# First attention layer of a two-layer cross-attention kernel: the weighted sum moved to directly behind the scores, all three probability groups turned and split in their own slot

## What is computed

```python
a = _layer_norm(audio_kv, ln_gamma, ln_beta)
Q = (hidden_states @ Wq.T).reshape(B, Tt, HEADS, HEAD_DIM).transpose(0, 2, 1, 3)
K = (a @ Wk.T).reshape(B, Ta, HEADS, HEAD_DIM).transpose(0, 2, 1, 3)
V = (a @ Wv.T).reshape(B, Ta, HEADS, HEAD_DIM).transpose(0, 2, 1, 3)
scores = jnp.einsum('bhtd,bhsd->bhts', Q, K) * scale
scores = jnp.where(mask, scores, jnp.float32(-jnp.inf))
attn = jax.nn.softmax(scores, axis=-1)
out = jnp.einsum('bhts,bhsd->bhtd', attn, V)
return hidden_states + jnp.tanh(gate) * (out.reshape(B, Tt, D) @ Wo.T)
```

## Time and profile before

| | us |
|---|---|
| median of three runs | 1791.48 (1789.04 to 1791.99) |
| the profiled execution | 1799.13 |
| its span | 1797.3 |
| TensorE busy in the span | 1672.9 (93%) |
| VectorE busy | 1203.6 (67%) |
| ScalarE busy | 1041.9 (58%) |
| GpSimd busy | 902.7 (50%) |
| DMA queue of SP, share of 16 engines | 28.4% |

### The profile page before, as it was taken

How to read it: one execution, slowest core, us unless ns; L and a number is a source line. 1 busy time by engine, 2 the same in 40 slices (tenths; PEclk the granted TensorE clock), 3 DMA queues, 4 the chain that set the end, 5 groups by cost and what they waited for, 6 DMA issues and landing times.

```text
span 1797.3 us, 36860 instructions
## 1 busy us (share of the span) xinstructions
PE 1672.9 (93%) x12520; PEld 1576.3 (88%) x12520; DVE 1203.6 (67%) x2340; ACT 1041.9 (58%) x2023; POOL 902.7 (50%) x655
## 2 busy tenths in 40 slices
PE   4788988997899999999999999999999999999997
PEld 3677877786789999999999987889999999999986
DVE  5577777777356766766766766466676677677673
ACT  2467766676264655656656555545665656556563
POOL 4456665542144545536535547453653554455483
PEclk8899999999699999999999999899999999999998
DMA  7967666746221111111211114221121121120031
GB/s 211 234 161 183 180 173 177 179 115 167 73 81 62 54 50 37 64 41 36 70 35 36 70 32 131 62 85 37 36 70 36 35 70 36 36 70 1 2 91 40
DMA packets 109995, 150.81 MB, mean 84 GB/s; under 512 B 25540, under 2 KB 95684, under 8 KB 109828
## 3 DMA queue, kind: packets, MB, share of 16 engines
q1 hardware_dynamic: 108484, 142.45, 28.4%
q10 hardware_dynamic: 1344, 6.19, 1.0%
HBM read 108.32 MB, written 3.42 MB: 62 GB/s over the span
## 4 chain that ended last, share of the span: by engine, by line
PE 67%; DVE 10%; ACT 3%; issue 2%; SPq 1%; POOL 1%; DMA 1%; ACTq 0%; DVEq 0%; POOLq 0%
PE ps L770 12%; PE ps L772 11%; PE ps L771 11%; PE ps L1025 7%; PE ps L1029 7%; PE ps L1027 7%; PE ps L960 2%; DVE ar L1866 2%; PE ps L1005 2%; PE ps L992 1%; DVE neg L1742 1%; PE ps L853 1%; PE ps L870 1%; DVE ar L1911 1%; ACT prob L1299 1%
## 5 line engine op out<-in xcount | busy, mean ns | idle before, releaser
L722 POOL TENSOR_TENSOR rr<-ar,rr 125x512 fp32r<-125x512 f32 x336 | 455.3, 1387 | 406.6 <-ACT rr L1483 398.7
L1025 PE MATMUL ps<-cx,rr 125*128 125x258 f32 x1344 | 396.6, 295 | 0.0
L1029 PE MATMUL ps<-cx,rr 125*128 125x258 f32 x1344 | 379.6, 282 | 0.0
L1027 PE MATMUL ps<-cx,rr 125*128 125x256 f32 x1344 | 379.3, 282 | 0.0
L770 PE MATMUL ps<-rr,ct 128*125 128x256 f32 x1152 | 329.6, 286 | 4.5 <-DVE ar L1911 2.7
L772 PE MATMUL ps<-rr,ct 128*125 128x256 f32 x1152 | 324.7, 282 | 0.0
L771 PE MATMUL ps<-rr,ct 128*125 128x256 f32 x1152 | 324.7, 282 | 0.0
L1470 ACT ACTIVATE ar<-ar 125x512 f32<-125x512 f32 x336 | 208.5, 626 | 84.5 <-DVE ar L1911 59.4
L1027 PEld LDWEIGHTS ps<-cx,rr 125*128 125x128 f32 x1344 | 254.9, 190 | 0.0
L1029 PEld LDWEIGHTS ps<-cx,rr 125*128 125x128 f32 x1344 | 254.8, 190 | 0.0
L1025 PEld LDWEIGHTS ps<-cx,rr 125*128 125x128 f32 x1344 | 253.6, 189 | 0.1
(11 more groups left out here) (210 smaller groups left out, 3778.6 us busy)
## 6 DMA issues: line engine op xcount, KB each, us to landing
raw_t<-in_ctx_t SPq DMA_DIRECT2D x24, 1500.0 KB, 6.7
k<-khl SPq DMA_DIRECT2D x192, 187.5 KB
raw<-in_ctx SPq DMA_DIRECT2D x16, 1500.0 KB
raw<-in_ctx SPq DMA_DIRECT2D x8, 1408.0 KB
raw<-stat_scratch ACTq DMA_DIRECT2D x7, 750.0 KB, 3.9
w_raw<-in_wq SPq DMA_DIRECT2D x32, 128.0 KB, 2.3
w_raw<-in_wk SPq DMA_DIRECT2D x32, 128.0 KB, 2.2
qo<-in_wqt SPq DMA_DIRECT2D x32, 128.0 KB, 3.2
```

Of the source, the lines that this page charges most:

```text
L722: pool.tensor_tensor(group(p[:, 1, :, :], u, k), x, f(group(p[:, 0, :, :], u, k)), ALU.subtract)\
L1025: pe.matmul(ps[:, bank, 0:D + 2], hi, cx[0:KC, c, 0:D + 2], start=c == 0, stop=False, skip_group_check=True)
L1027: pe.matmul(ps[:, bank, 0:D], hi, cx[0:KC, c, D + 2:CW], start=False, stop=False, skip_group_check=True)
L1029: mm = pe.matmul(ps[:, bank, 0:D + 2], lo, cx[0:KC, c, 0:D + 2], start=False, stop=c == CH - 1, skip_group_check=True)
```

## The change

In each slot, TensorE does the weighted sum of g-1 directly behind the scores of g+1, then turns 0 and 1 of g, then the key block, then the third turn of g itself, then the value block. ScalarE: value copy, output of g-1, high parts 0 and 1 of g, softmax of g+1, third high part of g, key copy. VectorE: maximum, low values, collapse, low parts 0 and 1, statistics (now at the end of slots 0, 1 and 2), third low part of g. GpSimd scales the second half of batch b+2 in slot 5 ahead of key block 5 instead of behind it. The statistics' turn in slot 3 goes back to bank 7 and waits for the collapse; in slot 4 the wait for its copy stands ahead of the weighted sum. Ahead of the slots, the statistics of batch 1 come behind the split of the first context, its turn behind key block 3 instead of 1, its spreading behind the last key copy instead of the fourth, and SP's load of raw for batch 1 behind all constants. Behind the slots, one third turn and one third high and low part go away, since they are done in their own slot.

```diff
@@ SP @@
                     n_const += 1
-                    if n_const == 10:
-
-                        sp.wait_ge(s["bn_done"], 3)
-                        load_raw(0, 1)
...
             constants()
+            sp.wait_ge(s["bn_done"], 3)
+            load_raw(0, 1)
@@ GpSimd @@
             def slot(b, t, n, kind):
                 if kind == "full" and t == 2:
                     variance(b + 2)
+                if kind == "full" and t == 5:
+                    scale(b + 2, 1)
...
-                    if t in (4, 5):
-                        scale(b + 2, t - 4)
+                    if t == 4:
+                        scale(b + 2, 0)
@@ TensorE @@
                 if t or later:
-                    transposes(g - 1, (t - 1) % SLOTS, 2)
+                    if t == 4 and kind == "full":
+                        pe.wait_ge(s["stat_row"], b + 3)
+                    weighted(b if t else b - 1, (t - 1) % SLOTS, g - 1, n if t else 1 - n)
+                transposes(g, t, 0)
+                transposes(g, t, 1)
                 if t in K_AT and kind != "plain":
                     u = K_N[t]
                     pe.wait_ge(s["zks"], 6 * (b + 1) + u)
-                    if t == 4 and kind == "full":
-                        pe.wait_ge(s["stat_row"], b + 3)
                     keys(b + 1, u, *K_AT[t], 5)
-                if t or later:
-                    weighted(b if t else b - 1, (t - 1) % SLOTS, g - 1, n if t else 1 - n)
-                transposes(g, t, 0)
-                transposes(g, t, 1)
+                transposes(g, t, 2)
                 if t == 3 and kind == "full":
-
-                    pe.wait_ge(s["zks"], 6 * (b + 1) + 4)
-                    turn_stats(b + 2, 5)
+                    pe.wait_ge(s["zoc"], g)
+                    turn_stats(b + 2)
...
                 keys(0, n, *K_FIRST[n], (5, 3)[n % 2])
-                if n == 1:
+                if n == 3:
                     pe.wait_ge(s["stat_row"], 1)
                     turn_stats(1)
...
             whole_batches(pe, slot, "full", "keys", "plain")
-            transposes(GT0 - 1, SLOTS - 1, 2)
             weighted(B - 1, SLOTS - 1, GT0 - 1, 1)
@@ ScalarE @@
-                if t or later:
-                    high_probs(g - 1, 2)
                 if u_last is not None and (t or later) and not (kind == "plain" and t):
...
-                if t in K_AT and kind != "plain":
-                    u = K_N[t]
-                    act.wait_ge(s["zkl"], 6 * (b + 1) + u - 4)
-                    keys(b + 1, u, 5)
+                if t or later:
+                    output(g - 1)
+                high_probs(g, 0)
+                high_probs(g, 1)
                 if kind == "full" and t == 4:
                     spread_stats(b + 2)
...
                     softmax(n if t < SLOTS - 1 else 1 - n, (t + 1) % SLOTS, g + 1)
-                if t or later:
-                    output(g - 1)
-                high_probs(g, 0)
-                high_probs(g, 1)
+                high_probs(g, 2)
+                if kind == "full" and t == 3:
+                    turn_stats(b + 2)
+                if t in K_AT and kind != "plain":
+                    u = K_N[t]
+                    act.wait_ge(s["zkl"], 6 * (b + 1) + u - 4)
+                    keys(b + 1, u, 5)
...
                 keys(0, n, (5, 3)[n % 2])
-                if n == 1:
+                if n == 3:
                     turn_stats(1)
-                if n == 3:
-                    spread_stats(1)
+            spread_stats(1)
@@ VectorE @@
-            for k in range(3):
-                load_stats(1, k)
             for jc in range(DH):
...
                 low(ct[:, 1, :, v], raw_t[:, :, v], ct[:, 0, :, v]).then_inc(s["zcv"], 1)
+            for k in range(3):
+                load_stats(1, k)
...
-                if t or later:
-                    low_probs(g - 1, 2)
                 if u_last is not None and (t or later) and not (kind == "plain" and t):
                     values(b + 1 if t else b, u_last, 1 - n if t else n, 6)
-                if t == 0 and later:
-                    reciprocals(b - 1, 1 - n)
-                if kind == "full" and t in (1, 2):
-                    load_stats(b + 2, t)
-                if kind == "plain" and t == SLOTS - 1:
-                    reciprocals(b, n)
                 if t or later:
                     collapse(b if t else b - 1, (t - 1) % SLOTS, g - 1)
                 low_probs(g, 0)
                 low_probs(g, 1)
-                if kind == "full" and t == 0:
-                    load_stats(b + 2, 0)
+                if t == 0 and later:
+                    reciprocals(b - 1, 1 - n)
+                if kind == "full" and t < 3:
+                    load_stats(b + 2, t)
+                if kind == "plain" and t == SLOTS - 1:
+                    reciprocals(b, n)
+                low_probs(g, 2)
```

More of the change, by code:

```diff
@@ L776, in _, with turn_stats @@
             drain(pe, 1)
-            def turn_stats(b, bank=7):
+            def turn_stats(b):
                 pe.wait_ge(s["std_ready"], 2 * b + 2)
-                pe.transpose(ps[0:CH, bank, 256:256 + P], mv[:, 1, :], ident[:, :]).then_inc(s["stat_t"], 1)
+                pe.transpose(ps[0:CH, 7, 256:256 + P], mv[:, 1, :], ident[:, :]).then_inc(s["stat_t"], 1)
             pe.wait_ge(s["w0_lo"], 1)
@@ L1252, in _, with turn_stats @@
             high(xs[:, 0, :, :], xt[:, :, :]).then_inc(s["x_hi"], 1)
-            def turn_stats(b, bank=7):
+            def turn_stats(b):
                 act.wait_ge(s["stat_t"], b + 1)
-                act.activation(mv_row[:, :], ps[0:CH, bank, 256:256 + P], ACT.Copy).then_inc(s["stat_row"], 1)
+                act.activation(mv_row[:, :], ps[0:CH, 7, 256:256 + P], ACT.Copy).then_inc(s["stat_row"], 1)
                 wait_apart(act, s["stat_row"], b + 1)
@@ L1354, in slot @@
                     softmax(n if t < SLOTS - 1 else 1 - n, (t + 1) % SLOTS, g + 1)
-                if t or later:
-                    output(g - 1)
-                high_probs(g, 0)
-                high_probs(g, 1)
+                high_probs(g, 2)
[5 more added lines that the diff above has]
+                    keys(b + 1, u, 5)
                 if kind == "full":
-                    if t == 3:
-                        turn_stats(b + 2, 5)
                     if t == 6:
@@ L1403, in _ @@
             whole_batches(act, slot, "full", "keys", "plain")
-            high_probs(GT0 - 1, 2)
             output(GT0 - 1)
@@ L1798, in _ @@
             whole_batches(dve, slot, "full", "keys", "plain")
-            low_probs(GT0 - 1, 2)
             collapse(B - 1, SLOTS - 1, GT0 - 1)
```

## The result

The changed kernel takes 1800.89 us, the median of 20 runs (1791.79 to 1809.42); the kernel before 1791.03 (20 runs, 1788.19 to 1798.48). The ratio is 1.0045, with an interval of 1.0028 to 1.0062: slower by 8 us by the ratio and by 9.9 us by the medians, where 1784.6 was forecast and the range ended at 1797. A second measurement further down gives 1.0056 [1.0035, 1.0078].

The account below looks back on a forecast made before the run. TensorE plus 28.8 us of idle time was taken to bound the slots, then a loop outside them. Start +2.5, loop -7.5, batch 6 +1.2 and batch 7 -3.1 gave -6.9: 1784.6 from 1791.48, range 1777 to 1797.

Parts of the forecast that it names:

- I leave them as they are in the sum: Last two windows, batches 6 and 7: TensorE's missing clock shares, 1.7 and 3.6 us, were kept unchanged.
- Start, "I take +2.5": Ahead of the slots: later statistics of batch 1 delay the start by 2.5 us, bounds 0 and 5.5.
- Key blocks 2 to 5 wait: Ahead of the slots: GpSimd's third context split moves from 36.13 to 41.7, and these blocks wait for it.
- Loop, -7.5: Batch 0's slot 3 to batch 6's slot 1: 275.1 us instead of 282.56.
- T: Time from SP's load of raw to GpSimd's key block 1, read as 25.1 to 28.1 us and taken as unchanged.
- 21.5 + T: Length per batch of the loop outside the slots: 16.8 from statistics' turn to load, 4.7 for block and variance, plus T.
- The paragraph on the rule against it: TensorE's clock: an array that idled runs at half clock until busy again; missing shares are 1.7 and 3.6 us.
- the clock falls where TensorE waits most: Last two windows: the trace's clocks of 0.96 and 0.92 were read as agreeing with the half-clock rule.
- rival (d): TensorE's clock: added idle time drops it, and the missing 5.3 us double, giving 1790; chance 8%.
- rival (b): Loop through raw and k3 gets longer, up to 3.3 us a batch in T, giving 1801; chance 24%.
- Batch 6, +1.2: Batch 6: 43.6 us instead of 42.41, with a 3 us stall for k3 before batch 7's scores.
- Batch 7, -3.1: Batch 7 and the tail: 42.4 us instead of 45.49, with slots of 5.18.

Follow-up runs that it names:

- cut3: Changed kernel with the old order ahead of the slots, GpSimd's variance ahead of key block 1, and the last batch's stacks 0 to 3 released by key block 4: 1783.08, ratio 0.9945.
- cut3b: The same kernel as cut3, measured once more: 1781.85 us, ratio 0.9951 to the kernel before.
- cut2late: Changed kernel with batch 1's variance behind GpSimd's first key block, the slots' variance ahead of key block 1, and earlier last stacks: 1781.61 us, ratio 0.9946.
- oldstart: Changed kernel with the order ahead of the slots of the kernel before: 1795.4 us, ratio 1.0023 to the kernel before.
- newstart: Kernel before with only the changed order ahead of the slots: 1798.55 us, ratio 1.0036 to the kernel before.
- latevar1: Changed kernel with GpSimd's variance of batch 1 moved from ahead of its third context split to behind its first key block: 1791.79 us, ratio 1.0011.
- earlyvar: Changed kernel with GpSimd's variance in the slots queued ahead of key block 1 instead of behind it: 1791.65 us, ratio 1.0005 to the kernel before.
- busyplain: cut3 with eight needless identity turns on TensorE in each of batch 7's slots 0 to 6: 1779.17 us, ratio 0.9922 to the kernel before.
- startvar: Changed kernel with the old order ahead of the slots and GpSimd's variance ahead of key block 1, without earlier last stacks: 1786.29 us, ratio 0.996.
- the second group: Runs of cut3, startvar, newstart and one further kernel beside the kernel before on one chip; ratios 0.9945, 0.996, 1.0036 and 1.0098.

## Why the prediction was wrong

**The step that failed.** The forecast put new waits of TensorE into its sum and left the clock out of it: "I leave them as they are in the sum". Of the 13.3 us between the forecast's -6.9 and the marks' +6.4, the lower clock behind waits, counted by the slots, is 2.35 us in the loop and 4.6 in batch 7 (three slots of 6.7 instead of 5.2), together about half. The rest is waiting itself: the loop's long laps (2.2 us, and 1.1 that the formula misses), a start mis-sized by 1.2, and small differences in batches 6 and 7. How far the losses can be undone is shown by runs (cut3, cut3b, cut2late); the clock's share is read from one profile and only argued.

**The order itself was read right.** The weighted sum's waits are gone, plain slots are 5.18, slot 4 5.42 (5.24 forecast), slots with keys and values 6.1 to 6.3 (6.15), batch 6 41.0 without its stall (40.7). With three edits beside it the order is worth 0.5% (0.9945, 0.9951, 0.9946). What was forecast is thus there, but the change doesn't reach it: three waits, each for something on GpSimd's or SP's list, together took 1% back (the two on GpSimd's list are measured singly, the one for k3 isn't told apart from nothing).

**Start, "I take +2.5": mis-sized, the place named.** VectorE's and GpSimd's scalings of the first context now begin together and take 4.41 and 3.31 us where VectorE's took 2.30 before; the statistics so ended at 40.8 and not 39.0, the third split came at 43.98 and not 41.7. "Key blocks 2 to 5 wait" stood there with no price: 6.87 us of idle TensorE, with the next key matmuls at the lower clock. The marks say +3.7, the runs 0.22% (oldstart), 0.36% (newstart) and 0.34% (latevar1), 4 to 6 us.

**Loop, -7.5: the formula held nearly, its price for a wait did not.** With the T of the changed kernel's own trace, 21.5 + T gives 50.1, 49.7 and 48.0 for batches 2, 3 and 5, and the slots give 47.45 for the other two (46.95 forecast): 242.7 for five, where 240.5 was forecast and 246.1 measured. Of the 3.4 left, 2.35 is the clock: slot 4 at 6.68 and 6.53. The paragraph on the rule against it asked whether the clock falls more in batches 6 and 7, where it already did; it fell in the loop too, at 1.00 before, where the forecast itself put new waits. Its reading that "the clock falls where TensorE waits most" was wrong as well: in the earlier trace rows TensorE is idle for 10% of the first window, at 1.00, and for 7% of the second, at 0.96. What came is rival (d), its 5.3 us against about 7, partly in a place it did not name, beside what rival (b) calls "the loop is longer", but not because T grows (26.7 in the mean, where it decides from 27.9); a single T of 28 costs 2 to 3 us and a T of 25 gives nothing back, since the slots then bind. A mean T in a sum hides this.

**Batch 6, +1.2: about right** (1.7), in part by luck. The stall for k3 was 1.9, not 3, and slot 7 behind it took 7.07 us and not the 6.2 of earlyvar, at the lower clock, which the sum didn't have. From SP's first stack (405.40) to these scores (410.33) it is 4.9 us, where issue and landing had been taken as 5.8.

**Batch 7, -3.1: wrong sign, +2.8.** The count of slots was right: 31.0 us for slots 0 to 5 in cut3b and busyplain, 31.25 before. In the changed kernel it was 35.6 and 36.9, by three and four slots at the lower clock. In the 18 profiles this stretch takes 30.5 to 31.3 in the three that keep the old order throughout, and 31.0 to 37.1 in the thirteen with the new one in batch 7 too. The stall for k3 ahead of it neither suffices nor is needed: the eight of the thirteen that have it took 31.1 to 36.9 (startvar, with a stall of 1.9, ran at full clock), the five without it 31.0 to 37.1 (cut2late). What sets the lower clock off there is open; busyplain speaks, weakly, for the idle time in its own slots.

**The clock in the timed runs.** Over the change's 20 runs, the mean clock is 0.968 to 0.977 with a mean of 0.973; over the 20 runs of the kernel before in the second group it is 0.974 to 0.980, mean 0.977. Over all timed runs, within one kernel, a mean clock lower by 0.001 goes with 1.35 us more. By that the missing 0.004 is some 5 of the 8 to 10 us. It is a correlation, since idle time and lower clock come together, and it isn't the whole price: earlyvar is 7 us faster than the changed kernel with a mean clock of 0.9735, higher by 0.0006 only. The Trainium skill (TensorE: Matmul & The Clock Gate, HAM oscillation — how this bites in real kernels) says that a wait which recurs in a loop, when it is long enough, throttles the array each time anew. The traces agree only in part: the clock fell behind the statistics' turn in four waits (1.81 to 2.83 us) and not in three others (1.57, 2.10 and 2.21).

## What to carry to other kernels

When an order is tightened until a loop outside it binds, price each new wait of TensorE with the work that may run at half clock behind it: here 1.2 us behind a wait of 2.4, where the clock fell. Take the slack per batch and not in the mean, since a short lap of the loop gives nothing back. And look down each in-order queue for one cheap instruction that waits ahead of something urgent: a single variance in GpSimd's list cost 0.34% ahead of the slots, and another 0.40% inside them. Moving it pays only in the order that needs it: in the kernel before, the second move cost 0.32%.

## What was not expected of the hardware

The length of a wait alone doesn't say whether the clock falls behind it: 1.81 us did it once and 2.21 did not. And in batch 7, where TensorE is busy 21.8 of 31.0 us and its waits are 0.93 us at most but for one of 1.51 in slot 0, the clock stayed full in one execution of cut3 and was 0.90 in another. Eight matmuls a slot that compute nothing shorten no step there, yet the kernel with them had the highest mean clock of its timed runs (0.9805) and the lowest time of all.
